# One set of statistics for the input's and the first layer's normalization, the input's applied by Pool at the end of a pass

## The reference

```python
def _layernorm(x, axis=-1, eps=1e-05):
    m = jnp.mean(x, axis=axis, keepdims=True)
    v = jnp.var(x, axis=axis, keepdims=True)
    return (x - m) / jnp.sqrt(v + eps)

def _ln(x, w, b):
    m = x.mean(-1, keepdims=True)
    v = ((x - m) ** 2).mean(-1, keepdims=True)
    return (x - m) * jax.lax.rsqrt(v + 1e-06) * w + b

h = _layernorm(x)                     # the input's normalization
for l in range(4):
    xn = _ln(h, ln1_w[l], ln1_b[l])   # a layer's first normalization
    h = h + _attn(xn, ...)            # 16 heads of 8, causal, relative positions
    fn = _ln(h, ln2_w[l], ln2_b[l])
    h = h + gelu(fn @ W1[l].T + b1[l]) @ W2[l].T + b2[l]
x = x + h
```

## Time and profile before

| | |
|---|---|
| median of 3 runs | 2396.32 us (2392.58 to 2398.49) |
| the profiled execution's own time | 2396.09 us |
| its span, first to last instruction | 2394.1 us |
| PE busy | 2283.0 us (95%), 31360 instructions |
| DVE busy | 2023.1 us (85%), 5071 instructions |
| ACT busy | 1838.9 us (77%) |
| POOL busy | 1147.2 us (48%) |

### The profile page before, as it was taken

The page is one execution under the profiler, slowest core; times in us unless marked ns, Lnnn a source line. Parts: engine busy times, 40 slices in busy tenths (PEclk is TensorE's granted clock), DMA queues, the critical chain, the costliest instruction groups (busy, mean ns, idle before and its releaser), DMA issues. The chain is left out here.

```text
span 2394.1 us, 83247 instructions
## 1 busy us (share of the span) xinstructions
PE 2283.0 (95%) x31360; PEld 1974.5 (82%) x31360; DVE 2023.1 (85%) x5071; ACT 1838.9 (77%) x2869; POOL 1147.2 (48%) x2089
## 2 busy tenths in 40 slices
PE   4899999999999999999999999999999999799998
PEld 3688888888888888888888888888888888677776
DVE  6799999888888888888888888888888886677774
ACT  2588888888888888888888888888888888655554
POOL 4355555555544455555454455555444553333332
PEclk8899999999999999999999999999999999899999
DMA  5434433333333333333333333333343331001000
GB/s 124 105 99 116 108 89 81 88 92 92 88 90 94 90 88 88 90 92 92 89 89 97 90 83 91 91 92 92 89 107 87 88 91 51 21 27 28 28 23 19
DMA packets 227432, 196.05 MB, mean 82 GB/s; under 512 B 29024, under 2 KB 225760, under 8 KB 227040
## 3 DMA queue, kind: packets, MB, share of 16 engines
q1 hardware_dynamic: 227040, 190.73, 30.0%
HBM read 14.46 MB, written 4.19 MB: 8 GB/s over the span
## 5 line engine op out<-in xcount | busy, mean ns | idle before, releaser
L1019 DVE TENSOR_REDUCE rowmax<-bank 128x4 f32<-128x1024 f32 (+1 forms) x768 | 914.7, 1219 | 102.5 <-PE bank L583 74.2
L824 ACT ACTIVATE probs<-bank 128x1024 f32<-128x1024 f32 x768 | 738.3, 1024 | 78.6 <-PE bank L643 78.2
L583 PE MATMUL bank<-kstack,qstack 62*128 62x256 f32 (+1 forms) x4096 | 417.9, 301 | 7.0 <-DMA qstack<-base 7.0
L643 PE MATMUL bank<-qstack,kstack 64*128 64x128 f32 (+1 forms) x4096 | 423.3, 299 | 0.0
L865 ACT ACT_TABLE_LOAD x256 | 328.4, 1283 | 4.5
L583 PEld LDWEIGHTS bank<-kstack,qstack 62*128 62x128 f32 x4096 | 317.3, 193 | 7.5 <-issue 7.5
L643 PEld LDWEIGHTS bank<-qstack,kstack 64*128 64x128 f32 x4096 | 316.2, 191 | 0.0
L605 PE MATMUL bank<-maskT_half,pick_half 64*128 64x128 bf16 (+1 forms) x3072 | 267.4, 241 | 22.3 <-DVE rowmax L1019 10.5
L545 PE MATMUL bank<-mask_half,pick_half 64*128 64x128 bf16 (+1 forms) x3072 | 268.9, 243 | 7.6 <-DVE h_all L1054 2.9
L732 PE MATMUL bank<-w,hidden 128*128 128x128 f32 x2048 | 271.7, 276 | 3.1 <-ACT hidden L874 3.1
L663 PE MATMUL bank<-probs,v_pad 128*32 128x256 f32 x4096 | 271.1, 382 | 1.1 <-DVE v_tok L1000 1.1
(11 more groups left out here) (154 smaller groups left out, 5259.6 us busy)
## 6 DMA issues: line engine op xcount, KB each, us to landing
qstack<-base SPq DMA_DIRECT2D x768, 128.0 KB, 2.5
kstack<-base SPq DMA_DIRECT2D x384, 128.0 KB, 2.5
turn_x<-turn_c SPq DMA_DIRECT2D x512, 32.0 KB, 1.9
qstack<-maxrows SPq DMA_DIRECT2D x256, 16.0 KB
out<-ot SPq DMA_DIRECT2D x16, 256.0 KB, 2.4
h_all<-in_x SPq DMA_DIRECT2D x7, 512.0 KB, 5.5
xin<-in_x SPq DMA_DIRECT2D x14, 256.0 KB, 3.2
w<-in_w SPq DMA_DIRECT2D x8, 256.0 KB, 3.3
```

What stands on the lines that cost most here:

```text
L583: last = pe.matmul(bank[:, b0 + b, i * wide:(i + 1) * wide], qstack[rows, r, p0 + i, t * 128:(t + 1) * 128], kstack[rows, r, p0 + i, 0:wid ...
L643: last = pe.matmul(bank[:, b0 + b, i * wide:(i + 1) * wide], kstack[rows, r, p0 + i, kt * 128:(kt + 1) * 128], qstack[rows, r, p0 + i, q0: ...
L824: act.activation(probs[:, k], bank[:, A_BANK[k]:A_BANK[k] + 2, :], ACT.Exp, scale=SCALE).then_inc(exp_done[k], 1)
L1019: dve.tensor_reduce(rowmax[:, n % 2, t, :, p0:p0 + heads], bank[:, M_BANK[k]:M_BANK[k] + 2, :].rearrange("p b (h c) -> p b h c", h=heads), ...
```

## The change

`stats_0`, `apply_0`, `power_0` and their buffers are gone. For the 32 jobs of the first layer `stats_1(n)` now reads the raw rows of x, once they have landed. Pool's `power_in(n)` makes two factors from the one variance: the input's own and the product of both normalizations, with one more TENSOR_SCALAR and with a power of four columns where there were two. `apply_1(n)` uses the product. The input's own normalization, which h_all needs for the residual, is written by Pool: `normalize_in(n)` is two TENSOR_SCALAR of 128x128, at the end of Pool's slot n-1, behind `turned`. mv1 and rstd1 get two buffers each, so that the next job's statistics don't overwrite what `normalize_in` reads.

```diff
             def stats_1(n):
-                dve.wait_ge(ln0_done, min(n, B - 1) // PER + 1)
+                if n < B:
+                    dve.wait_ge(x_landed[sum(start <= n for start in X_STARTS) - 1], 16)
                 at_least(dve, h2_ready, n - B + 1)
-                norm_stats(stats1, mv1, stats1_done, mv1_ready, n)
+                at_least(dve, ln0_done, min(n - 1, B))
+                norm_stats(stats1, mv1[:, n % 2], stats1_done, mv1_ready, n)
...
-                if s == -1:
-                    stats_0(1)
...
-                    apply_0(1)
...
-                if s % PER == 0 and LN0_FIRST <= s // PER + 2 < B // PER:
-                    apply_0(s // PER + 2)
-                if s % PER == 1 and LN0_FIRST <= s // PER + 3 < B // PER:
-                    stats_0(s // PER + 3)
...
+            def power_in(n):
+                pool.wait_ge(mv1_ready, n + 1)
+                pool.tensor_scalar(ve1[:, T:2 * T], mv1[:, n % 2, :, 1], EPS_IN, None, ALU.add)
+                pool.tensor_scalar(ve1[:, 0:T], mv1[:, n % 2, :, 1], 1 + EPS_LAYER, EPS_LAYER * EPS_IN, ALU.mult, ALU.add
+                                   ).then_inc(ve1_ready, 1)
+                pool.wait_ge(ve1_ready, n + 1)
+                pool.tensor_tensor(rstd1[:, n % 2], ve1[:], expo[:, 0:2 * T], ALU.pow).then_inc(rstd1_ready, 1)
+
+            def normalize_in(n):
+                pool.wait_ge(xn1_ready, T * (n + 1))
+                for t in range(T):
+                    tile = h_all[:, n, t]
+                    last = pool.tensor_scalar(tile, tile, mv1[:, n % 2, t, 0:1], rstd1[:, n % 2, T + t:T + t + 1],
+                                              ALU.subtract, ALU.mult)
+                last.then_inc(ln0_done, 1)
...
             def add_row(n, rows, landed, dmas, read_sem, value, added_sem):
 
                 pool.wait_ge(read_sem, value)
+                if n < B:
+                    pool.wait_ge(ln0_done, n + 1)
...
-                if live(s + 1):
-                    power(ve1, mv1, rstd1, mv1_ready, ve1_ready, rstd1_ready, s + 1)
-                if s > 0 and s % PER == 1 and LN0_FIRST <= s // PER + 3 < B // PER:
-                    power_0(s // PER + 3)
+                if live(s + 1) and 0 < s + 1 < B:
+                    power_in(s + 1)
+                if live(s + 1) and s + 1 >= B:
+                    power(ve1, mv1[:, (s + 1) % 2], rstd1[:, (s + 1) % 2], mv1_ready, ve1_ready, rstd1_ready, s + 1)
...
-                if s == -1:
-                    power_0(1)
-                    power_0(2)
+                if live(s + 1) and s + 1 < B:
+                    normalize_in(s + 1)
```

More of the change, by code:

```diff
@@ L64 @@
 STACK_DMAS = 2 * NP
-PER = 2
-LN0_FIRST = 2
+EPS_IN, EPS_LAYER = 1e-5, 1e-6
 LEAD, LAG = 1, 6
@@ L239, in layers_program @@
         expo = sb("expo", [128, 16])
[L241 to L244, removed]
         stats1 = sb("stats1", [128, T, 6])
-        mv1 = sb("mv1", [128, T, 2])
-        ve1 = sb("ve1", [128, T])
-        rstd1 = sb("rstd1", [128, T])
+        mv1 = sb("mv1", [128, 2, T, 2])
+        ve1 = sb("ve1", [128, 2 * T])
+        rstd1 = sb("rstd1", [128, 2, 2 * T])
         xn1 = sb("xn1", [128, T, D])
@@ L303, in layers_program @@
         apart_dve, apart_pool = (sem(f"apart_{e}") for e in ("dve", "pool"))
[L305 to L308, removed]
         ln0_done = sem("ln0_done")
@@ L930, in cast_masks @@
                                 ).then_inc(consts_cast, 1)
[L932 to L951, removed]
             def norm_stats(stats, mv, stats_sem, mv_sem, n):
@@ L969, in stats_1 @@
             def stats_1(n):
-                dve.wait_ge(ln0_done, min(n, B - 1) // PER + 1)
+                if n < B:
+                    dve.wait_ge(x_landed[sum(start <= n for start in X_STARTS) - 1], 16)
                 at_least(dve, h2_ready, n - B + 1)
-                norm_stats(stats1, mv1, stats1_done, mv1_ready, n)
+                at_least(dve, ln0_done, min(n - 1, B))
+                norm_stats(stats1, mv1[:, n % 2], stats1_done, mv1_ready, n)
             def apply_1(n):
-                norm_apply(xn1, mv1, rstd1, rstd1_ready, xn1_turned, xn1_ready, n)
+                norm_apply(xn1, mv1[:, n % 2], rstd1[:, n % 2], rstd1_ready, xn1_turned, xn1_ready, n)
             def stats_2(n):
@@ L1159, in _ @@
         def _(pool):
-            def power_0(g):
-                pool.wait_ge(mv0_ready, g + 1)
-                at_least(pool, ln0_done, g)
-                pool.tensor_scalar(ve0[:], mv0[:, :, 1], 1e-5, None, ALU.add).then_inc(ve0_ready, 1)
-                pool.wait_ge(ve0_ready, g + 1)
-                pool.tensor_tensor(rstd0[:], ve0[:], expo[:, 0:PER * T], ALU.pow).then_inc(rstd0_ready, 1)
+            def power_in(n):
[12 more added lines that the diff above has]
+                last.then_inc(ln0_done, 1)
             def power(ve, mv, rstd, mv_sem, ve_sem, rstd_sem, n):
                 pool.wait_ge(mv_sem, n + 1)
-                pool.tensor_scalar(ve[:], mv[:, :, 1], 1e-6, None, ALU.add).then_inc(ve_sem, 1)
+                pool.tensor_scalar(ve[:, 0:T], mv[:, :, 1], EPS_LAYER, None, ALU.add).then_inc(ve_sem, 1)
                 pool.wait_ge(ve_sem, n + 1)
-                pool.tensor_tensor(rstd[:], ve[:], expo[:, 0:T], ALU.pow).then_inc(rstd_sem, 1)
+                pool.tensor_tensor(rstd[:, 0:T], ve[:, 0:T], expo[:, 0:T], ALU.pow).then_inc(rstd_sem, 1)
             def split_qkv(ly):
@@ L1253, in _ @@
             pool.wait_ge(expo_filled, 1)
-            power_0(0)
+            power_in(0)
             pool.wait_ge(w0_landed, 16)
```

## The result

| | before | after |
|---|---|---|
| median | 2397.11 us (12 runs, 2392.58 to 2400.29) | 2406.59 us (12 runs, 2400.91 to 2412.59) |
| span of the profiled execution | 2394.1 us | 2404.6 us |
| DVE busy | 2023.1 us | 1993.4 us |
| POOL busy | 1147.2 us | 1189.9 us |

The ratio is 1.0042, with a 95% interval of 1.003 to 1.0053. The forecast was 2380 us, 2373 to 2391. The time fell on the other side of the kernel before, close to the time that the first rival had (2405.5 us).

The account below looks back on a forecast made before the run. PE, delayed 0.55 us a slot by DVE's row maxima, was taken as the bound, with PE's own work behind it. 11.5 + 5.8 + 1.5 - 2.7 = 16.1 us gained, giving 2380.0 us, range 2373 to 2391.

Parts of the forecast that it names:

- the first rival: Pool's TENSOR_SCALAR at the wait of `up`: dear passes, a pair 1.65 us, make PE wait; slower, 2405.5 us; chance 0.06.
- What bounds the kernel: Jobs 7 to 27: DVE's row maxima delay PE 0.55 us a slot; behind that, PE's own 15.33 us.
- Step 1: Jobs 6 to 27: without DVE's input-normalization bursts the slot falls to 15.33 us; 21 x 0.55 = 11.5 us gained.
- Step 2: Kernel start: first xn 4.0 us sooner, then 2.1 of turn_s delay gone; 5.8 us gained, bounds 4.0 and 6.1.
- Step 3: First slots: one or two of four or five bursts lie where DVE and PE bind; 1.5 us gained, 1.2 to 2.4.
- the 3 us kept for the clock: First 120 us: PE's slow-clock spells may shift either way; 3 us on both sides of the range, nothing in the sum.
- Step 4: End of Pool's slot: normalize_in's pair, 0.67 us, exceeds 0.59 us of room before PE's `up`; 2.7 us lost.
- a chance of 0.83 for faster: Whole kernel: chance of being over 0.3% faster, under 2389.1 us; within 0.11, slower 0.06.
- What costs nothing: Pool's `power_in` with wider power, covered by Pool's 3 us wait, and the waits on `ln0_done`: no loss.
- Port contention: Pool's passes and DVE's hold each other, 0.3 us a slot; 9.6 us lost, 2389.6; chance 0.04.

Follow-up runs that it names:

- late kernel: The changed kernel with normalize_in moved from the end of Pool's slot to its idle wait ahead of xn1_split, one slot later; 2381.78 us, ratio 0.9937.
- the two kernels with the same work there: Against the late kernel: one added Pool instructions in slots 72 to 91, 2380.65 us; the other moved weight splits into Pool's idle stretch, 2378.50 us.
- the kernel that priced instructions: The late kernel plus one or two scratch Pool instructions a slot in slots 72 to 91, in the idle stretch; 2380.65 us in its one execution.
- the half dose: The changed kernel with the first tile's pass left at the end of Pool's slot, the second's moved ahead of xn1_split; 2390.97 us, ratio 0.9974.
- the late kernel with x in twos: The late kernel with x loaded two sequences at a time in even slots and three weight loads moved; 2371.49 us, ratio 0.9898.

## Why the prediction was wrong, point by point

**What bounds the kernel:** right. 15.33 us is PE's own slot, 0.55 us were lost to DVE's row maxima, and without the bursts and the passes in the chain the slots came down to 15.33.

**Step 1, the steady slots, 11.5 us:** the mechanism was right, the size depended on what I had not looked for. With the passes in their late place 4.0 us came back between jobs 7 and 27 (5.4 and 7.6 in the traces of the two kernels with the same work there), since loads of x, hidden before, then became the bound; with the loads thinned out it was 10.9, where 20 x 0.55 = 11.0 were forecast. The prediction said "if nothing new is late" and named only Pool. In the changed kernel, with PE waiting for Pool, the bursts were worth 0.41 us a slot.

**Step 2, the start, 5.8 us:** 5.2. Its rows, to be read against the earlier trace rows:

```profile
7.59 1.21 DVE L934 TENSOR_SCALAR xn<-h_all,mv,rstd 128x128 f32<-128x128 f32 x2 [1.81 <-POOL rstd L1129]
...
11.05 0.53 DVE L1097 TENSOR_TENSOR b_cols<-b_cols,u_cols 128x4 f32<-128x4 f32 x1 [1.24 <-DMA b_v<-in_b_v]
...
14.50 0.48 DVE L964 SCALAR_TENSOR_TENSOR turn_s<-bank,b_cols,turn 128x256 f32<-128x256 f32 x1
```

The first xn starts at 7.59, as worked out (7.6). It takes 1.21 us, not 0.60, while Pool casts the weights; turn_s comes at 14.50 instead of 13.8. These 0.6 us are what the step lacks.

**Step 3, the fill, 1.5 us:** not settled. In the late kernel's trace job 6's mark comes 7.05 us sooner, for steps 2 and 3 together 7.3 forecast. In the trace of the kernel that priced instructions, with the same work up to there, it is 8.6, at a granted clock of 0.98 instead of 0.85, and without the passes 5.5, at 0.83. So the agreement is partly luck, and the 3 us kept for the clock are about what the clock can move. In the changed kernel it is 4.5: the passes take part of it back, which the prediction, that counted them from slot 6 on only, left out.

**Step 4, Pool's work, 2.7 us: this is the step that failed.** Its place, its room and its rule were right: room 0.59, measured 0.58 by the half dose; a pair of 1.53, and 0.04 to 0.05 by which the instruction ahead is drawn out, less 0.58 is 1.0, and the slots went from 15.33 to 16.34. In 26 slots that is some 26 us instead of 2.7. The price of the pass was wrong. The prediction took a slope from "the casts give (617 - 397)/256 = 0.86 ns a column", came to 331 ns, and "since both factors are read per partition" took 360; it is 797. The slope was borrowed from another operation. The rows of the same instruction, with 223 and 233 ns, gave 5 ns a column; I used them for the rival and gave that 0.06, since "casts and copies stream at 0.86 ns a column". Their 853 ns are near the 797, but by luck: those rows have one operation with its number in the instruction, and that form takes 550 ns at 128 columns, not 853. No row of the kernel before had the price of this form. The rival's sum of 2405.5 us, 1 us under the measured time, is luck in part too: its pair of 1.65 us is 0.07 too dear, some 2 us in all, and neither the passes' cost in the fill nor the loads' 1.8 us are in it. And the price ruled over the sign: the break-even that the prediction had worked out, 1.29 us a pair, lay inside the bounds of 0.53 to 1.41 that it gave itself, so a chance of 0.83 for faster was not to be had from them.

**What costs nothing:** right. The late kernel has the wider power and the new waits, and runs the slots of jobs 18 to 27 at 15.33.

**Port contention:** right for the steady slots. In the changed kernel and the late one the passes meet no DVE work there but row maxima from PSUM, as the prediction had it: in the changed kernel these take 1.22 us each with a pass beside them (48 of them) and without. So the rule of Perfetto Trace Analysis, section "Optimizing Scalar/DVE Operations" of the Trainium skill, that GpSimd and DVE share an SBUF port and offloading between them might not help, is not tested by the passes, but for one in the late kernel with x in twos: there a CAST of maxparts beside a pass took 249 ns, where the others took 171 in the mean. At the start something like it shows: the 1.21 us above, with Pool's casts and a TENSOR_TENSOR at the same time, are in agreement with it, and so are the four L947 of the kernel before, 1.73 us beside Pool's work in the earlier trace rows and 1.11 us at 16.28, where Pool does little. That the port is the cause no run shows.

## What to carry to other kernels

When work is moved to an engine that is half idle, find the chain in which its new place stands, and the engine's long waits: the same two instructions cost 25 us at the end of Pool's slot and nothing in the engine's wait ahead of xn1_split. The price of an instruction with no row of its own form is not known: here another operation's slope gave 360 ns and the small rows of the same operation 853, for 797. Where break-even lies within the bounds of such a price, either measure it or forecast both signs. And a bound that is removed uncovers the next: look beyond the engines, at transfers that came late in the shadow of the old wait.

## What the runs showed of the hardware

On Pool a TENSOR_SCALAR of 128 columns took 806 ns with two operations and factors from columns, 608 with one. A TENSOR_TENSOR of the same columns took 462 (a product), and 402 with a broadcast column as its second input (a difference), so for one operation the form with two inputs was the cheaper one. GPSIMD Engine Reference of the Trainium skill, "Elementwise — side-by-side cycle accounting", has bodies of up to two operations bound by the port at 1.03 cycles an element. That agrees here with the casts (0.86 ns a column, as the prediction worked out) and not with TENSOR_SCALAR, of which the section gives no figure: 3.35 ns a column.
